# Value products of a cross-attention and expert-FFN kernel: three of eight in high and low parts, their result kept once in head order, and six kinds of DMA issued elsewhere

## The reference, cut to what matters

```
lat = layer_norm(layer_norm(x)) * w_l + b_l ;  f = layer_norm(ctx) * w_m + b_m
kv  = concat([f, lat])                       # 128 rows of 128
q, k, v = lat @ Wq, kv @ Wk, kv @ Wv         # per head
p   = softmax(q k^T * scale + mask)          # mask on the 64 context rows
x1  = x + concat_heads(p @ v) @ Wo
x2  = layer_norm(x1)
out = x1 + shared_ffn(x2) + sum over the top 2 of 8 experts, weighted by sigmoid gates
```

## Time and profile before

| | |
|---|---|
| median of three runs | 1117.17 us |
| profiled execution, its own time | 1118.87 us |
| its span, first to last instruction | 1117.1 us |
| granted TensorE clock, mean | 0.991 |
| PE busy | 1076.3 us (96%) |
| DVE busy | 928.3 us (83%) |
| ACT busy | 789.0 us (71%) |
| POOL busy | 617.0 us (55%) |

### The profile page before, as it was taken

One profiled execution on the slowest core, in us unless ns is written; L12 is line 12 of the kernel. 1 busy time (PEld: TensorE's weight loads), 2 busy tenths in 40 slices (PEclk: granted clock), 3 DMA queues, 4 the chain that ended last, 5 costly groups with the idle time before them and its releaser, 6 DMA issues.

```text
span 1117.1 us, 28209 instructions
## 1 busy us (share of the span) xinstructions
PE 1076.3 (96%) x7720; PEld 939.3 (84%) x7720; DVE 928.3 (83%) x4095; ACT 789.0 (71%) x2924; POOL 617.0 (55%) x717
## 2 busy tenths in 40 slices
PE   6899999999999999999999999999999999999986
PEld 5688888888888888888888888888888888888765
DVE  3878988888988888988888888888898888888856
ACT  4777777767777776777776777777777777777631
POOL 5554655565656565655555556556565556554421
PEclk9999999999999999999999999999999999999989
DMA  5454555555565545555555655555555554555541
GB/s 153 128 175 152 171 171 166 153 155 162 168 176 171 160 146 167 171 171 165 157 155 159 172 170 169 168 156 158 165 168 171 174 153 153 163 168 160 158 121 34
DMA packets 248717, 176.81 MB, mean 158 GB/s; under 512 B 29424, under 2 KB 215408, under 8 KB 248560
## 3 DMA queue, kind: packets, MB, share of 16 engines
q1 hardware_dynamic: 247376, 173.96, 52.6%
q10 hardware_dynamic: 1184, 1.05, 0.3%
HBM read 103.35 MB, written 71.56 MB: 157 GB/s over the span
## 4 chain that ended last, share of the span: by engine, by line
PE 61%; SPq 14%; DMA 9%; DVE 8%; issue 5%; ACT 2%; POOL 0%; DVEq 0%; POOLq 0%; ACTq 0%
PE bank L861 14%; PE bank L874 12%; PE bank L816 9%; PE bank L818 9%; PE bank L817 9%; SPq L335 8%; DMA pT<-probsT_dram 8%; PE bank L822 5%; SPq L328 2%; SPq L351 2%; DVE probsT L687 2%; DVE logits L672 1%; SPq L369 1%; ACT cT_hi L528 1%; ACT probs L558 1%
## 5 line engine op out<-in xcount | busy, mean ns | idle before, releaser
L454 POOL TENSOR_TENSOR probs<-probs,rdenom 128x512 f32<-128x512 f32 x256 | 266.7, 1042 | 339.8 <-DVE rdenom L681 335.4
L558 ACT ACTIVATE probs<-logits,neg_max 128x128 f32<-128x128 f32 x1024 | 398.8, 396 | 0.9 <-DVE neg_max L672 0.9
L874 PEld LDWEIGHTS bank<-kvT,tT 128*128 128x128 f32 x2048 | 268.9, 192 | 120.5 <-issue 102.2
L861 PE MATMUL bank<-pT,kv_f 128*128 128x512 f32 x512 | 267.5, 604 | 16.5 <-DMA pT<-probsT_dram 16.0
L874 PE MATMUL bank<-kvT,tT 128*128 128x128 f32 x2048 | 270.5, 275 | 0.0
L672 DVE CUSTOM_DVE_ANT_0 logits<-bank,mask_add 128x128 f32<-128x128 f32 x1024 | 232.5, 282 | 6.1 <-PE bank L874 5.9
L717 DVE TENSOR_TENSOR cT_lo<-bank,cT_hi 128x512 fp32r<-128x512 f32 x256 | 175.1, 684 | 60.5 <-ACT cT_hi L528 60.5
L528 ACT CAST cT_hi<-bank 128x512 fp32r<-128x512 f32 x256 | 150.1, 586 | 94.7 <-PE bank L861 94.6
L558 ACT ACTIVATION_READ_ACCUMULATOR probs<-logits,neg_max 128x1 f32 x1024 | 197.7, 193 | 0.0
L513 ACT ACTIVATE h_tanh<-bank 128x256 f32<-128x256 f32 x160 | 61.6, 385 | 179.1 <-PE bank L818 176.7
L687 DVE STREAM_TRANSPOSE probsT<-probs 128x512 f32<-128x512 f32 x256 | 175.9, 687 | 0.5 <-issue 0.5
(11 more groups left out here) (102 smaller groups left out, 1986.1 us busy)
## 6 DMA issues: line engine op xcount, KB each, us to landing
probsT_dram<-probsT SPq DMA_DIRECT2D x256, 256.0 KB, 2.2
pT<-probsT_dram SPq DMA_DIRECT2D x1024, 64.0 KB, 2.2
gates<-gates_dram SPq DMA_DIRECT2D x62, 256.0 KB, 4.2
kv_raw<-in_ctx SPq DMA_DIRECT2D x32, 128.0 KB, 2.8
kv_raw<-in_x SPq DMA_DIRECT2D x32, 128.0 KB, 2.9
mask_raw<-in_mask_BxS_ik SPq DMA_DIRECT2D x32, 128.0 KB, 3.7
x_res<-in_x SPq DMA_DIRECT2D x32, 128.0 KB, 2.6
out<-out_sb SPq DMA_DIRECT2D x32, 128.0 KB, 2.1
```

The source lines that it names most:

```text
L454: nc.gpsimd.tensor_tensor(by_pair, by_pair, rdenom[n][:, :].unsqueeze(2).unsqueeze(3).broadcast_to([P, PAIRS, P // QUAD, QUAD]), ALU.mult) ...
L558: nc.scalar.activation(probs[c % 4][:, :, r, :], logits[c % 2][:, r, :].rearrange("p (c k) -> p c k", k=QUAD), ACT.Exp, bias=neg_max[c % 2 ...
L861: nc.tensor.matmul(C_ps[c % 2][:, :], kv_f[g % 3][:, kl % 4, :], pT[c % 3][:, :], start=True, stop=True).then_inc(C_in_psum, 1)
L874: last = nc.tensor.matmul(S_ps[c % 2][:, P * r:P * (r + 1)], tT[:, kl % 4, hd:hd + 2, :], kvT[g % 2][:, kl % 4, :], start=True, stop=True)
```

## The change

The value products of halves 1, 2 and 3 of each group (steps 5, 6 and 7 on PE) are no longer one float32 product but three float32r products of high and low parts. ACT copies the loaded probabilities to `pT_hi`, POOL subtracts to get `pT_lo`, both in step c+3, before the copy of `cT_hi` and before POOL's own `keys` work of that step. POOL also splits `kv_f` into `kv_hi` and `kv_lo` (two more steps of `keys`, in step 1 of the next frame). `cT_hi` and `cT_lo` are kept once instead of twice, in head order: ACT and DVE write them through a permuted pattern (`by_quad`), and a new semaphore `W_front_done` frees the front half. The gates' store moves from SP (steps 5 and 6) to ACT (end of step 6); the gates' load moves from step 0 of the next frame to step 7; raw rows from step 7 to step 2; mask from 1 to 3; `x_res` from 2 to 3; output from 3 to 4. The buffer `h` is placed elsewhere in SBUF.

Constants and patterns:

```diff
-        KV_STEPS = 6
+        KV_STEPS = 8
+        SPLIT_HALVES = (1, 2, 3)
...
-            hh, r, odd = hd // 8, hd % 8 // 2, hd % 2
-            return cT.rearrange("p b t (o a r q) -> p b t o a r q", o=2, a=2, r=PAIRS)[:, :, hh, odd, :, r, :]
+            return cT.rearrange("p b t (h q) -> p b t h q", h=8)[:, :, hd // 8, hd % 8, :]
+        def by_quad(row):
+            return row.rearrange("p (r a q) -> p a r q", r=PAIRS, q=QUAD)
```

SP's frame:

```diff
-                    if k == 0 and has(j, p, 3, NG + 1):
-                        sp.wait_ge(gates_stored, 64 * (i - 2))
+                    if k == 2 and has(j, p, -2, NG - 4):
+                        load_kv(j, p + 3)
+                    if k == 3 and has(j, p, -1, NG - 3):
+                        load_mask(j, p + 2)
+                    if k == 3 and has(j, p, 0, NG - 1):
...
+                    if k == 7 and has(j, p, 2, NG):
+                        sp.wait_ge(gates_stored, 64 * (i - 1))
+                        after(sp, h_routed_done, NT * (i - 2))
                         for a in range(2):
                             sp.dma_start(gates[FH * a:FH * (a + 1), :, :],
...
-                    if k in (5, 6) and has(j, p, 2, NG):
-                        sp.wait_ge(gate_step, GATE_STEPS * (i - 1))
-                        for a in (0, 1) if k == 5 else (2, 3):
-                            sp.dma_start(gates_dram.rearrange("e (t a q) -> e t a q", t=TT, a=P // QUAD)[:, :, a, :],
-                                         g_denseT[QUAD * a:QUAD * a + E, :, :]).then_inc(gates_stored, 16)
```

POOL, in `keys` and in its frame:

```diff
+                if 7 in steps:
+                    after(pool, C_in_psum, HALVES * (g - 2))
+                    pool.wait_ge(kv_step, step + 6)
+                    nc.gpsimd.tensor_copy(kv_hi[g % 3][:, :, :], kv_f[g % 3][:, :, :]).then_inc(kv_step, 1)
+                if 8 in steps:
+                    pool.wait_ge(kv_step, step + 7)
+                    nc.gpsimd.tensor_tensor(kv_lo[g % 3][:, :, :], kv_f[g % 3][:, :, :], kv_hi[g % 3][:, :, :].bitcast(fp32),
+                                            ALU.subtract).then_inc(kv_step, 1)
...
+                    if has_split(e - 3):
+                        c = e - 3
+                        n = split_before(c)
+                        pool.wait_ge(pT_hi_ready, n + 1)
+                        nc.gpsimd.tensor_tensor(pT_lo[n % 2][:, :], pT[c % 3][:, :], pT_hi[n % 2][:, :].bitcast(fp32),
+                                                ALU.subtract).then_inc(pT_lo_ready, 1)
+                    if has(j, p, -1, NG - 2):
+                        keys(j, p + 1, {1: (7, 8)}.get(k, ()))
```

ACT's frame:

```diff
+                    if has_split(e - 3):
+                        c = e - 3
+                        n = split_before(c)
+                        act.wait_ge(pT_loaded[c % 3], 64 * (c // 3 + 1))
+                        after(act, C_in_psum, c - 1)
+                        nc.scalar.copy(pT_hi[n % 2][:, :], pT[c % 3][:, :]).then_inc(pT_hi_ready, 1)
                     if has_half(e - 4):
...
-                            after(act, W_in_psum, g - 1)
-                        nc.scalar.copy(cT_hi[g % 2][:, kl % 4, kl // 4, :], C_ps[c % 2][:, :]).then_inc(cT_hi_ready, 1)
+                            after(act, W_front_done, g)
+                        if kl == 4:
+                            after(act, W_in_psum, g)
+                        nc.scalar.copy(by_quad(cT_hi[:, kl % 4, kl // 4, :]),
+                                       C_ps[c % 2][:, :].rearrange("p (a r q) -> p a r q", r=PAIRS, q=QUAD)).then_inc(cT_hi_ready, 1)
...
+                    if k == 6 and has(j, p, 2, NG):
+                        act.wait_ge(gate_step, GATE_STEPS * (i - 1))
+                        after(act, gates_loaded, 32 * (i - 2))
+                        for a in range(P // QUAD):
+                            nc.scalar.dma_start(gates_dram.rearrange("e (t a q) -> e t a q", t=TT, a=P // QUAD)[:, :, a, :],
+                                                g_denseT[QUAD * a:QUAD * a + E, :, :]).then_inc(gates_stored, 16)
```

PE's frame (DVE's `cT_lo` changes as ACT's `cT_hi` does):

```diff
+                        if has_split(c):
+                            pe.wait_ge(pT_lo_ready, split_before(c) + 1)
+                        else:
+                            pe.wait_ge(pT_loaded[c % 3], 64 * (c // 3 + 1))
...
+                        if has_split(c):
+                            n = split_before(c)
+                            last = matmul3(C_ps[c % 2][:, :], kv_hi[g % 3][:, kl % 4, :], kv_lo[g % 3][:, kl % 4, :],
+                                           pT_hi[n % 2][:, :], pT_lo[n % 2][:, :])
+                        else:
+                            last = nc.tensor.matmul(C_ps[c % 2][:, :], kv_f[g % 3][:, kl % 4, :], pT[c % 3][:, :],
+                                                    start=True, stop=True)
+                        last.then_inc(C_in_psum, 1)
...
+                            if hd == H // 2 - 1:
+                                last.then_inc(W_front_done, 1)
```

More of the change, by code:

```diff
@@ L63, in xattn_moe_ffn_kernel @@
         kv_f = [sb(f"kv_f{n}", [P, GB, D]) for n in range(3)]
+        kv_hi = [sb(f"kv_hi{n}", [P, GB, D], f32r) for n in range(3)]
+        kv_lo = [sb(f"kv_lo{n}", [P, GB, D], f32r) for n in range(3)]
         kvT = [sb(f"kvT{n}", [P, GB, P]) for n in range(2)]
@@ L78, in xattn_moe_ffn_kernel @@
         pT = [sb(f"pT{n}", [P, PAIRS * P]) for n in range(3)]
+        pT_hi = [sb(f"pT_hi{n}", [P, PAIRS * P], f32r) for n in range(2)]
+        pT_lo = [sb(f"pT_lo{n}", [P, PAIRS * P], f32r) for n in range(2)]
         attnT = sb("attnT", [P, GT])
@@ L120, in xattn_moe_ffn_kernel @@
             wT = [su(f"wT{n}", [P, H // 2, D]) for n in range(3)]
-            su("unused", [P, 5 * H * DH])
+            su("unused", [P, H * DH])
             w13_stage = [su(f"w13_stage{n}", [P, (NT + 1) * P]) for n in range(2)]
-        cT_hi = [sb(f"cT_hi{n}", [P, GB, 2, PAIRS * P], f32r) for n in range(2)]
-        cT_lo = [sb(f"cT_lo{n}", [P, GB, 2, PAIRS * P], f32r) for n in range(2)]
+        cT_hi = sb("cT_hi", [P, GB, 2, PAIRS * P], f32r)
+        cT_lo = sb("cT_lo", [P, GB, 2, PAIRS * P], f32r)
+        h = [sb(f"h{n}", [P, NT + 1, GT]) for n in range(2)]
         banks = [es.enter_context(nc.psum_tensor(f"bank{n}", [P, 512], fp32)) for n in range(8)]
@@ L241, in query_chunk_before, with split_before, has_split @@
             return query_chunk(j, p, k - 1)
+        def split_before(c):
+            return len(SPLIT_HALVES) * (c // HALVES) + sum(k < c % HALVES for k in SPLIT_HALVES)
+        def has_split(c):
+            return has_half(c) and c % HALVES in SPLIT_HALVES
         def head_columns(cT, hd):
-            hh, r, odd = hd // 8, hd % 8 // 2, hd % 2
-            return cT.rearrange("p b t (o a r q) -> p b t o a r q", o=2, a=2, r=PAIRS)[:, :, hh, odd, :, r, :]
+            return cT.rearrange("p b t (h q) -> p b t h q", h=8)[:, :, hd // 8, hd % 8, :]
+        def by_quad(row):
+            return row.rearrange("p (r a q) -> p a r q", r=PAIRS, q=QUAD)
         def query_bank(c, i):
@@ L346, in frame @@
                         load_probs(e - 2)
-                    if k == 0 and has(j, p, 3, NG + 1):
-                        sp.wait_ge(gates_stored, 64 * (i - 2))
-                        after(sp, h_routed_done, NT * (i - 3))
+                    if k == 2 and has(j, p, -2, NG - 4):
[3 more added lines that the diff above has]
+                    if k == 3 and has(j, p, 0, NG - 1):
+                        after(sp, x1_step, 3 * (i - 2) + 1)
+                        sp.dma_start(x_res[p][:, :, :],
+                                     x.rearrange("b s d -> (b s) d")[bass.ds(GT * i, GT), :].rearrange("(t q) d -> q t d", q=P)
+                                     ).then_inc(x_res_loaded[p], 16)
+                    if k == 4 and has(j, p, 4, NG + 2):
+                        store_out(i - 1)
+                    if k == 7 and has(j, p, 2, NG):
+                        sp.wait_ge(gates_stored, 64 * (i - 1))
+                        after(sp, h_routed_done, NT * (i - 2))
                         for a in range(2):
```

34 lines of the change are left out of this document (12 added, 22 removed).

## The result

The changed kernel has a median of 1143.3 us (1140.2 to 1148.6) against 1117.2 us for the kernel before, run beside it: 1.022 times as long, 95% interval 1.0185 to 1.0255. The forecast was 1126 us with a range up to 1140: the direction is right, the size is not. The profiled execution took 1140.28 us, 1138.6 of it span.

A forecast was written before the change was run, and what follows sets the result against it. PE bound the kernel, with the wait for `attnT` next: 33.01 + 0.15 + 0.43 - 0.17 + 0.10 = 33.52 us a frame against 33.22, 8.7 us more over 29 frames, 1127.6 less 1.7: 1126 us, range 1092 to 1140.

The forecast's parts named there:

- 0.30 x 29 = 8.7 us more: Full frames: 33.52 us predicted against 33.22 before, over 29 frames.
- idle time such as the 1.62 us before 533.09: ACT's idle time in steps 4 and 5, said to hide copies that would otherwise push the exponentials by 0.5 us each.
- ACT as issuer of the gates' store: ACT, end of step 6: four issues of 2.92 us delay `tT` and PE's queries; taken at 0.10 us a frame.
- Landing and copy: ACT's step 6: `pT_hi` awaits its block ahead of `attnT`, making the attention transposes 0.15 us late.
- Held `g_dense`: DVE's `g_dense` waits out POOL's subtraction, delayed by `pT_lo`; the block transpose and `attnT` come 0.43 us later.
- price of `pT_lo`: POOL's step 4: the subtraction lies between 1.04 and 1.28 us; 1.04, the division's time, was taken.
- float32r passes of 512 columns: PE's value products: 0.23 us a pass, three passes 0.69 us against 0.86, gaining 0.17 us a product.
- late landings: PE's waits for probabilities not yet landed: 16.0 us in all, counted as 16.0/31 a frame if gone.
- 0.51 forecast: PE's gain a frame from three value products in float32r, 0.17 us each.
- Third rival: On PE, a 512-column float32r pass costs as much as a float32 one: 34.40 us a frame, 1151 us; chance 0.05.
- second rival: ACT's issues of the gates' store cover nothing: 0.33 us more a frame, 1136 us; chance 0.18.
- first rival: PE stays the bound, `attnT` being ready for the attention transposes: 32.19 us a frame or more, priced at 1098; chance 0.35.

The follow-up runs named there:

- e5: Changed kernel with the first group's eight value products left whole: 1138.6 us, ratio 1.020 to the kernel before.
- e12: Changed kernel with only halves 1 and 2 split, from the third group on, and the last frame's gates moved as before the change: 1102.9 us, ratio 0.985.
- e6: Changed kernel with the last gates' store and load (frame NG) back on SP at their old places: 1138.9 us, ratio 1.019 to the kernel before.
- e8: Changed kernel with half 3 alone split, halves 1 and 2 whole: 1127.8 us, ratio 1.009 to the kernel before.
- e9: Changed kernel, all three halves split, with ACT making half 3's `pT_hi` behind `attnT` instead of ahead of it: 1110.2 us, ratio 0.992.
- e1: Changed kernel with no half split: head order, single `cT` and moved DMAs alone; 1110.4 us, ratio 0.994 to the kernel before.
- e13: Changed kernel with its three halves split only from the third group on and the last frame's gates moved as before the change: 1136.4 us, ratio 1.013.
- e11: Changed kernel with only halves 1 and 2 split, from the second group on, and the last frame's gates moved as before the change: 1105.1 us, ratio 0.988.
- e7: Changed kernel with half 1 alone split, halves 2 and 3 whole: 1108.1 us, ratio 0.992 to the kernel before.

## Why the prediction was wrong

- **What failed: the sum's coverage.** "0.30 x 29 = 8.7 us more" prices the 29 full frames and takes the start and the end at nothing. Measured: 6.9 us at the start and 5.2 us in the tail, 12.1 of the 21.5 us between the two spans. At the start, the cover named for the copies ("idle time such as the 1.62 us before 533.09") is one of full frames; what waits behind `pT_hi` and `pT_lo` in the first two groups is PE itself (e5, e12). At the end it is the term "ACT as issuer of the gates' store", priced in full frames alone: the queue that took over the store is the one that is blocked there, behind a `tanh` that waits for PE (e6 gives 3.1 us back; of the other 2.1, 1.2 are slower products, the rest stays open). Nearly 5 more of the 17 us missed are no part of the mechanism: the sum took off 1.7 us because the execution profiled before stood that much above its median, and the one profiled after, 1140.3, stands 3.1 below its own, 1143.3.
- **The frame was right**, 33.52 predicted, 33.56 measured, and so was its chain: PE waits for `attnT`, `pT_hi` for a landing, and `g_dense` is held, each as named there. "Landing and copy", 33.01 + 0.15 - 0.17 in the frame followed, that is 33.20 in the mean, has half 3 alone at 33.15 (e8). "Held `g_dense`", 0.43, is 0.41 from e8 to the changed kernel (which also splits halves 1 and 2); the instruction itself went from 0.17 to a median of 0.66 us. The price of `pT_lo` was near its dear end, 1.29 us rather than the 1.04 taken. That the sum came within 0.04 us is in part luck: its terms were added to one frame of 33.01 and the sum was set against the mean of 33.22 (added to the mean, they give 33.73); 0.10 of it, the issues, was not there; and with `pT_lo` at its measured price the same working gives a hold of 0.67, where the median measured is 0.49.
- **float32r passes of 512 columns**: taken at 0.23 us from start to start, measured 0.23 (544.27 to 544.50). Third rival refuted. Where the wait is away the frame is 32.48 (e9), 0.74 less than before. 0.49 of this is there without any split (32.73 in e1), close to the 0.5 that I put on late landings. The three products give 0.25 in the mean and 0.5, near the 0.51 forecast, where nothing else is late: 13 of e9's 25 frames lie between 32.2 and 32.3 us, and nearly all of e1's at 32.7.
- **ACT's issues**: taken at 0.10 us, measured at nothing in the full frames. In the timeline of ACT, the exponentials and the issues run side by side:

```profile
551.94 0.67 ACTq L604 DMA_DIRECT2D gates_dram<-g_denseT  x1
552.07 0.41 ACT L597 ACTIVATE probs<-logits,neg_max 128x128 f32<-128x128 f32 x1
...
553.34 0.67 ACTq L604 DMA_DIRECT2D gates_dram<-g_denseT  x1
...
554.10 0.59 ACT L550 COPY tT<-bank 128x512 f32<-128x512 f32 x1 [0.39 <-issue]
```

  Only the `tT` copy is held, by 0.39 us, and PE's queries don't wait for it between 150 and 1030 us. The second rival falls. The Trainium skill (Perfetto Trace Analysis, section DVE / Act Engine Instruction), by which a sequencer is free once it has pushed an instruction, would have made this term nothing; this trace agrees.
- **The first rival**, PE as the bound, was one reordered copy away: e9's commonest frame is the 32.2 us that it named, its mean 32.48, and it was the place named for it, the wait before the transposes, that decided.
- **The range** ended at 1140 because its upper case was the issues on ACT; no case had the ends of the run in it.

## What to carry to other kernels

Price an edit at three places, not one: the full frames, the filling of the pipeline and its draining; a cover that hides a latency in the middle doesn't exist at the ends, and a transfer moved to a queue whose engine waits there shows. When a wait moves into an engine's queue, look at what stands behind it: a copy that waits for a DMA belongs behind the copies that don't. And a delay has a price only where something waits for its result, so follow it instruction by instruction to one that does.

## What the runs showed of the hardware

- Waits of PE were often followed by slower products: granted clock 0.50 after one of 2.34 us (e13), and after one of 4.01 us at the end of the changed kernel 20 expert products in 3.92 us, against 2.50 in the kernel before, after a wait of 1.59. There a late transfer was paid twice. The length of the wait does not settle it: after 2.15 us the 20 took 2.50 in e11, after 2.10 us 4.31 in e12, where the clock had been at 0.55 before.
- ACT's sequencer issues DMAs of 0.67 us each while its own exponentials run.
- A DVE instruction with two SBUF inputs that meets a POOL instruction can be held for 0.5 us at no cost to the kernel (e7, e9), or for the same 0.5 us at 0.41 us a frame, according to who waits for what follows it.
